# A fused cross-attention and routed-FFN block: value products in four blocks of three key tiles a batch in place of six of two

## The reference, cut to what matters

```python
x = x + tanh(g_xattn) * xattn(layernorm(x), ctx)          # 32 batches, 56 queries, 1500 keys, 16 heads of 8
x = x + tanh(g_ffn)   * ffn(layernorm(x))                 # router over 160 experts, 8 chosen, and a shared one

scores = einsum('bhtd,bhcd->bhtc', q, k) / sqrt(8)
attn   = softmax(scores)
out    = einsum('bhtc,bhcd->bhtd', attn, v)               # then @ Wo.T + bo
```

## Time and profile before

| what | value |
|---|---|
| median of 3 runs | 1142.51 us (1139.42 to 1143.39) |
| the profiled execution | 1137.02 us, of which 1135.5 us are its span |
| granted TensorE clock, mean | 0.984 |
| PE, DVE, ACT, POOL busy | 94%, 85%, 74%, 54% of the span |
| L1205, scores | 275.3 us busy, 1536 matmuls |
| L1224, maxima | 254.6 us busy, 672 matmuls |
| L1190, value products | 188.4 us busy, 6144 passes |
| L721, exponentials | 400.0 us busy, 768 instructions of 544 ns |
| L917, row maxima | 420.1 us busy, 672 instructions of 671 ns |

### The profile page before, as it was taken

One profiled execution on the slowest core, in us unless ns is written; L12 is line 12 of the kernel. 1 busy time (PEld: TensorE's weight loads), 2 busy tenths in 40 slices (PEclk: granted clock), 3 DMA queues, 4 the chain that ended last, 5 costly groups with the idle time before them and its releaser, 6 DMA issues.

```text
span 1135.5 us, 37967 instructions
## 1 busy us (share of the span) xinstructions
PE 1066.0 (94%) x12090; PEld 706.0 (62%) x12090; DVE 968.6 (85%) x1706; ACT 844.9 (74%) x1812; POOL 611.1 (54%) x1042
## 2 busy tenths in 40 slices
PE   3798999999999999989999999769999999999998
PEld 1375777777777777767777777534555555555554
DVE  4686888888888888888887887669999999999998
ACT  2575777777777777767777776648888888888887
POOL 5898888888888888888888988000000000000000
PEclk9898999999999999999999999889999999999999
DMA  7776977577576676665675642146777777767773
GB/s 158 156 170 160 189 164 178 133 189 161 135 191 148 158 183 140 165 170 139 168 177 138 164 109 66 42 134 199 228 225 238 234 227 228 237 232 226 226 238 118
DMA packets 201815, 197.05 MB, mean 174 GB/s; under 512 B 161999, under 2 KB 168207, under 8 KB 201782
## 3 DMA queue, kind: packets, MB, share of 16 engines
q1 hardware_dynamic: 188292, 174.14, 58.5%
q0 software_dynamic: 11520, 20.99, 6.3%
q10 hardware_dynamic: 1970, 1.49, 0.6%
HBM read 109.96 MB, written 12.55 MB: 108 GB/s over the span
## 4 chain that ended last, share of the span: by engine, by line
PE 56%; DVE 14%; POOL 12%; issue 10%; DMA 2%; SPq 2%; ACT 1%; POOLq 1%; DVEq 1%; ACTq 0%
PE bank L1389 15%; PE bank L1361 15%; PE bank L1190 7%; DVE part_max L917 6%; PE bank L1205 6%; PE bank L1224 6%; DVE rec L1044 3%; PE bank L1260 3%; PE bank L1248 2%; POOL q_st L623 2%; POOL ctx_parts L515 2%; POOL w_in L488 2%; POOL q_blk L605 1%; POOL w_in L490 1%; SPq L378 1%
## 5 line engine op out<-in xcount | busy, mean ns | idle before, releaser
L721 ACT ACTIVATE p_exp<-bank 125x448 f32<-125x448 f32 x768 | 400.0, 544 | 189.5 <-PE bank L1205 188.6
L917 DVE TENSOR_REDUCE part_max<-bank 128x1 f32<-128x500 f32 x672 | 420.1, 671 | 67.9 <-PE bank L1224 67.5
L1205 PE MATMUL bank<-q_st,k_stk 97*125 97x224 f16 x1536 | 275.3, 264 | 7.1 <-ACT p_exp L721 5.8
L1224 PE MATMUL bank<-kparts,q_blk 128*128 128x500 f16 x672 | 254.6, 382 | 14.6 <-DVE part_max L917 12.2
L1205 PEld LDWEIGHTS bank<-q_st,k_stk 97*125 97x125 f16 x1536 | 197.3, 139 | 71.4 <-ACT p_exp L721 15.5
L1389 PE MATMUL bank<-ctT,w_ring 128*128 128x448 f16 x960 | 235.0, 354 | 4.3 <-DVE ctT L1092 4.3
L798 ACT ACTIVATE ctT<-bank 128x448 f32<-128x448 f32 x320 | 173.7, 543 | 42.3 <-PE bank L1361 18.0
L1092 DVE TENSOR_TENSOR ctT<-k_stk,ctT 128x448 f16<-128x448 f32 x320 | 198.1, 619 | 0.6 <-ACT ctT L804 0.4
L1190 PE MATMUL bank<-p_exp,v_sb 125*25 125x168 f32 (+1 forms) x6144 | 188.4, 264 | 0.4 <-ACT p_exp L721 0.4
L804 ACT ACTIVATE ctT<-k_stk 128x448 f16<-128x448 f32 x320 | 181.7, 568 | 6.7 <-DVE k_stk L1086 4.4
L1361 PE MATMUL bank<-q_hi,w_ring 128*128 128x448 f16 x640 | 174.6, 355 | 3.2 <-ACT k_stk L787 3.2
(11 more groups left out here) (157 smaller groups left out, 1234.2 us busy)
## 6 DMA issues: line engine op xcount, KB each, us to landing
v_sb<-c_scratch SPq DMA_DIRECT2D x114, 448.0 KB, 4.0
k_stk<-kparts SPq DMA_DIRECT2D x384, 93.8 KB, 3.2
ctx_in<-in_ctx_dram SPq DMA_DIRECT2D x30, 672.0 KB
k_stk<-c_scratch SPq DMA_DIRECT2D x38, 448.0 KB, 3.9
w_scratch<-w_out POOLq DMA_DIRECT2D x80, 128.0 KB, 2.8
w_in<-in_L_ffn_w_gate_dram POOLq DMA_DIRECT2D x160, 32.0 KB, 2.6
w_in<-in_L_ffn_w_down_dram POOLq DMA_DIRECT2D x80, 64.0 KB, 3.2
ctx_in<-in_ctx_dram SPq DMA_DIRECT2D x30, 78.0 KB
```

Source lines behind the costliest of these rows:

```text
L721: act.activation(p_exp[0:KP, j % PR, f * 448:(f + 1) * 448], ST[f][0:KP, 0:448], ACT.Exp).then_inc(exp_done, 1)
L917: v.reduce_max(part_max[:, i // NCH, i % NCH:i % NCH + 1], SM[i % NSM][:, 0:CK], axis=AX.X).then_inc(sm_maxed, 1)
L1205: last = pe.matmul(ST[f][0:KP, (g % 2) * GC:(g % 2 + 1) * GC], k_stk[0:97, u, g, j * KP:(j + 1) * KP], q_st[0:97, u, g, :, :].rearrange("p ...
L1224: pe.matmul(SM[i % NSM][:, 0:CK], rows, kparts[:, u, 0, c * CK:(c + 1) * CK], start=True, stop=True).then_inc(sm_done, 1)
```

## The change

`LAG` goes from 3 to 4, and a new constant `BLOCK = 3` sets how many tiles a block of value products takes.

```diff
-    LAG = 3
+    LAG, BLOCK = 4, 3
...
-                    if values_there and jv % 2:
-                        value_product(bv_, jv - 1)
-                        value_product(bv_, jv)
+                    if values_there and jv % BLOCK == BLOCK - 1:
+                        for j in range(jv - BLOCK + 1, jv + 1):
+                            value_product(bv_, j)
```

## The result

The changed kernel takes 1208.88 us (median of 4 runs, 1205.63 to 1210.06) where the kernel before takes 1140.97 beside it (4 runs, 1138.07 to 1143.39): a ratio of 1.060, 95% interval 1.057 to 1.062. The profiled execution took 1210.06 us with a span of 1208.5, which is 73.0 more than before. 1212 was forecast.

The account below looks back on a forecast made before the run. TensorE's issue order was taken to set the step. Terms summed to +2.41, taken as 2.40, over 29 steps 69.6, with the ends +71 us: 1212 predicted, 8-in-10 range 1194 to 1226.

Parts of the forecast that it names:

- slots 3, 5, 9: These slots lose their block but keep ScalarE's copy; way to the next second scores falls only to 2.07 or 2.04: -0.51.
- slot 11: Loses its block; way to slot 0's second scores becomes 2.07 in both kinds of step, -0.42 us in the mean.
- slots 1, 7: Their blocks of value products get a third tile at 0.39 each: +0.78 us a step on TensorE.
- slots 4, 10: Get a block of three they did not have, 1.38 each: +2.76 us a step.
- slot 8: TensorE's wait for VectorE after the reciprocal mostly goes, as VectorE catches up in a longer step: -0.30 us.
- refill: After a wait for an exponential the maxima chunk starts 0.24 behind its scores: +0.04 each, +0.10 a step taken.
- The round trip: Scores to exponential 0.47, second exponential 1.00 (values 0.97), next scores 0.60: next slot's second scores not before 2.07 (2.04).
- The count of steps: Steps 3 to 31 give 29 x 2.40 = 69.6; step 2 0, step 32 +1, end +1, hidden -1: +71.
- A: Rival: blocks' gain stays, no waits come in slots 3, 5 and 9; -0.78 a step, 1119 us. Chance 0.05.
- B: Rival: key copies hold TensorE up, value copies don't; slots 5 and 9 cost 0.25 each, 1180 us. Chance 0.08.
- C: Rival: late chunks in slots 4 and 10 delay VectorE for slots 8 and 9; +0.3 to +0.6 a step, 1225. Chance 0.12.
- D: Rival: the new waits lower TensorE's granted clock; streaming takes 3 us more a step, over 1290 us. Chance 0.02.

## Why the prediction was right, point by point

Lengths are differences of starts in TensorE's timeline, the mean of a step with and one without the output projection:

| term (us a step) | predicted | measured |
|---|---|---|
| slots 3, 5, 9: way 2.22, 2.22, 2.23 to 2.07, 2.06, 2.06 | -0.51 | -0.48 |
| slot 11: way 2.91 and 2.07 to 2.07 and 2.07 | -0.42 | -0.42 |
| slots 1, 7: 1.82 to 2.20 each | +0.78 | +0.76 |
| slots 4, 10, from their second scores on: 1.10 to 2.54, 0.84 to 2.27 | +2.76 | +2.87 |
| slot 8: 2.05 and 1.93 to 1.55 | -0.30 | -0.44 |
| refill (scores after a wait take longer to their chunk), beside what is in slots 4 and 10: slot 6, 1.42 to 1.47 | +0.10 | +0.05 |
| slot 0, from its second scores on: 1.12 and 1.15 to 1.41 and 1.15 | none | +0.15 |
| sum | +2.41 | +2.49 |

The sum is nearer than its terms. Slot 8 gave 0.14 more than forecast, and slot 0 took 0.15 that was not forecast; that these two cancel is luck. The other terms are off by 0.11 or less.

**The round trip.** It holds TensorE up where it was forecast, in slots 4, 6, 10 and 0, and in no other slot of a regular step. The first scores of these slots wait as well, but within the same way. The sum of its three parts, 2.07 and 2.04, met the measured 2.06 and 2.07 to 0.02. Between slot 11 and slot 0 it sets both kinds of step, as TensorE's timeline shows for one of each:

```profile
612.36 0.55 PE L1205 MATMUL bank<-q_st,k_stk 97*125 97x224 f16 x4
...
613.43 0.41 PE L1205 MATMUL bank<-q_st,k_stk 97*125 97x224 f16 x2 [0.37 <-ACT p_exp L721]
...
614.43 0.41 PE L1205 MATMUL bank<-q_st,k_stk 97*125 97x224 f16 x2
...
635.44 0.55 PE L1205 MATMUL bank<-q_st,k_stk 97*125 97x224 f16 x4
...
637.51 0.41 PE L1205 MATMUL bank<-q_st,k_stk 97*125 97x224 f16 x2
637.76 0.38 PE L1224 MATMUL bank<-kparts,q_blk 128*128 128x500 f16 x1
```

Without an output projection most of the wait stands ahead of slot 0's second scores, at its first ones and at the chunk between. With one TensorE's own work is 2.00, not the 1.92 of the prediction, so the round trip adds only 0.07 there.

**The blocks.** From the scores ahead of a block to the chunk behind it, less the 0.19 to 0.20 without one, it is 0.60 for one tile (in the kernel with blocks of one), 0.99 for two and 1.37 for three (1.38 was forecast): 0.385 a tile and 0.21 a block. That 0.21 fits the Trainium skill's statement, TensorEngine Tiling (Array Packing), Key Properties, that a change of tiling mode drains TensorE, though no run here separates a drain from anything else that a block's way in and out holds. Two blocks fewer a step save two of it, the 0.42 of the prediction. What outweighs it is that the blocks had covered a round trip of another engine.

**VectorE.** Its wait in slot 8 is gone but for 0.03, as the 0.23 from scores to chunk shows. The reason is not the prediction's, that VectorE catches up in a longer step. TensorE's timeline from the spread matmul to that chunk, in the kernel before and then in the changed one:

```profile
610.64 0.54 PE L1272 MATMUL bank<-o_raw,den_spread 128*128 128x224 f32 x2
...
613.85 0.38 PE L1224 MATMUL bank<-kparts,q_blk 128*128 128x500 f16 x1 [0.25 <-DVE part_max L917]
```

```profile
603.91 0.54 PE L1272 MATMUL bank<-o_raw,den_spread 128*128 128x224 f32 x2
...
606.89 0.35 PE L1205 MATMUL bank<-q_st,k_stk 97*125 97x224 f16 x2
607.12 0.39 PE L1224 MATMUL bank<-kparts,q_blk 128*128 128x500 f16 x1
```

It is 3.21 in both, so VectorE is no sooner. What changed is that TensorE has a third tile to multiply in slot 7 meanwhile. Its 0.38 fills what was a wait: it is paid in the row of slots 1 and 7 and comes back in that of slot 8, and that nothing hides the longer blocks was wrong for this one.

From slot 9 to slot 10 VectorE's late chunks lie within the wait for ScalarE, as the prediction left room for. TensorE's timeline there, one step later:

```profile
631.12 0.36 PE L1205 MATMUL bank<-q_st,k_stk 97*125 97x224 f16 x2
...
631.53 0.35 PE L1205 MATMUL bank<-q_st,k_stk 97*125 97x224 f16 x2
632.02 0.39 PE L1224 MATMUL bank<-kparts,q_blk 128*128 128x500 f16 x1
...
633.17 0.41 PE L1205 MATMUL bank<-q_st,k_stk 97*125 97x224 f16 x2 [0.19 <-ACT p_exp L721]
```

The chunk comes 0.49 after its scores instead of 0.20, but the way from 631.12 to 633.17 is 2.05.

**What was not forecast** is slot 0's 0.29 behind an output projection. This is read from the rows alone; no run tries it. The value projection behind the chunk of 637.76 shares its bank with the output projection, and VectorE reads that late, at 637.72, because its low part of the keys (L1035) waits for ScalarE's copy of slot 11. Before, it had waited for the output projection itself, and TensorE not for it. VectorE's timeline before, then after:

```profile
620.63 0.35 DVE L1027 SCALAR_TENSOR_TENSOR xt<-bank,tg,xt 112x128 f32 x1 [0.45 <-PE bank L1284]
```

```profile
637.06 0.74 DVE L1035 SCALAR_TENSOR_TENSOR kparts<-bank,bkc,kparts 128x500 f16<-128x500 f32 x1 [2.54 <-ACT kparts L776]
637.72 0.34 DVE L1027 SCALAR_TENSOR_TENSOR xt<-bank,tg,xt 112x128 f32 x1
```

**The count of steps.** Measured by the transposes, steps 3 to 31 grew by 67.5 together (69.6 less the hidden 1 was forecast): in two steps whose key projection came late before, the new waits hid in that, and these steps grew by 0.2 only. Step 32 added 1.2 and the end 1.8 (1 and 1 forecast), step 2 0.9 (0 forecast); what lies ahead of step 2 took 1.6 more, and why stays open. Sum 73.0.

**The rivals.** A fell with the first row of a wait. B: value copies hold TensorE up as long as key copies do (2.06 and 2.07). C did not come here; its wait in slot 8 came with `LAG = 3`, for want of a block in slot 7. D: the clock stayed at 1.00. What was only argued, and not tried, is that SP's and POOL's moved waits cost nothing; no row of the changed kernel speaks against it, and POOL's share of the chain that ended last fell from 12% on the page of before to 0% after.

## What to carry to other kernels

Work that looks free to move on the busiest engine may be the cover for a round trip of another one. Before moving it, measure the way scores, exponential, copy, next scores in the trace (it stands there wherever the cover happens to be missing, as in the first step of a pipeline), and count the places where the new order leaves it bare: one at most in the kernel before, four with the change, six with blocks of two a slot later, at some 0.55 to 0.85 us each (the way less TensorE's own work in it). When blocks move, move the other engine's copies with them, and look again at what waits behind a longer block. And when a wait goes, look whether the engine waited for got faster or the waiting one merely has more to do.

## What was not expected of the hardware

Putting a block directly ahead of the next slot's scores is not free: with the chunk issued first, scores that follow a block take 0.24 to their chunk where others take 0.19 to 0.20. Five slots a step pay that.
